# Two graph attention layers, a state space layer and an LSTM in one program: the borders between the layers rearranged

## Time and profile before

| | us |
|---|---|
| median of 3 runs | 4435.55 (4434.5 to 4436.84) |
| profiled execution, its own time | 4431.37 |
| its span | 4429.5 |
| TensorE, VectorE, ScalarE, GpSimd busy | 3978.7, 3492.4, 2881.1, 1199.0 |

### The profile page before, as it was taken

How to read it: one execution, slowest core, us unless ns; L and a number is a source line. 1 busy time by engine, 2 the same in 40 slices (tenths; PEclk the granted TensorE clock), 3 DMA queues, 4 the chain that set the end, 5 groups by cost and what they waited for, 6 DMA issues and landing times. The chain is left out here.

```text
span 4429.5 us, 143416 instructions
## 1 busy us (share of the span) xinstructions
PE 3978.7 (90%) x55570; PEld 2862.1 (65%) x55713; DVE 3492.4 (79%) x9562; ACT 2881.1 (65%) x7050; POOL 1199.0 (27%) x1032
## 2 busy tenths in 40 slices
PE   7999999996999999999997999978888888888882
PEld 4666666653666666666665877767777777777772
DVE  6999999995898889889886888856666666666666
ACT  6999999995888888888885767743333333333330
POOL 4777777862222222222222111000000000000000
PEclk9999999998999999999998999999999999999996
DMA  2222222211000000000002443311121111111115
GB/s 67 79 76 74 77 61 74 77 53 36 25 25 30 30 20 30 30 20 30 30 15 76 145 135 134 128 52 39 36 43 37 43 37 42 39 40 41 38 38 166
DMA packets 327038, 251.03 MB, mean 57 GB/s; under 512 B 172888, under 2 KB 291032, under 8 KB 324312
## 3 DMA queue, kind: packets, MB, share of 16 engines
q1 hardware_dynamic: 324824, 233.40, 18.2%
q10 hardware_dynamic: 1536, 8.39, 0.7%
HBM read 157.27 MB, written 67.12 MB: 51 GB/s over the span
## 5 line engine op out<-in xcount | busy, mean ns | idle before, releaser
L2578 PE MATMUL lstm_G_psum<-next_Whh,lstm_HT 128*32 128x192 f32 x8192 | 439.8, 333 | 238.6 <-DVE lstm_HT L2710 238.6
L2649 ACT ACTIVATE lstm_TC<-lstm_G_psum 128x192 f32<-128x192 f32 x512 | 169.6, 331 | 656.6 <-PE lstm_G_psum L2578 656.6
L1565 ACT ACTIVATE ssm_EX<-ssm_Z_psum,ssm_tok 128x256 f32<-128x256 f32 (+1 forms) x1024 | 371.7, 423 | 156.1 <-PE ssm_Z_psum L1396 86.3
L2570 PE MATMUL lstm_G_psum<-next_Wih,lstm_XT 128*32 128x192 f32 x8192 | 428.1, 327 | 0.0
L2578 PEld LDWEIGHTS lstm_G_psum<-next_Whh,lstm_HT 128*32 128x32 f32 x8192 | 214.4, 109 | 321.1 <-DVE lstm_HT L2710 287.9
L2697 DVE SCALAR_TENSOR_TENSOR lstm_AB<-lstm_TC 128x128 f32<-128x128 f32 x512 | 149.9, 293 | 310.0 <-ACT lstm_TC L2649 307.8
L616 ACT ACTIVATE g_PR<-g_S,g_nmax 128x512 f32<-128x512 f32 x512 | 368.7, 723 | 4.8 <-DVE g_nmax L751 4.8
L758 DVE COPY g_PT<-g_PT_psum 128x512 f32<-128x512 f32 x512 | 344.3, 683 | 25.4 <-PE g_PT_psum L485 20.6
L607 ACT ACTIVATE g_relu<-g_Z_psum,g_src 128x512 f32<-128x512 f32 x512 | 346.5, 684 | 19.3 <-PE g_Z_psum L478 19.3
L2872 POOL TENSOR_SCALAR lstm_rstd<-lstm_mv 128x4 f32<-128x4 f32 x32 | 7.2, 226 | 1277.8 <-DVE lstm_mv L2691 1277.8
L751 DVE CUSTOM_DVE_ANT_0 g_S<-g_Z_psum,g_relu 128x512 f32<-128x512 f32 x512 | 345.1, 683 | 8.8 <-ACT g_relu L607 7.3
(11 more groups left out here) (307 smaller groups left out, 10873.8 us busy)
## 6 DMA issues: line engine op xcount, KB each, us to landing
g_ADJ<-in_adj SPq DMA_DIRECT2D x64, 1024.0 KB, 7.4
x<-g_XO SPq DMA_DIRECT2D x64, 512.0 KB, 5.3
g_X<-in_x SPq DMA_DIRECT2D x32, 512.0 KB, 4.3
ssm_X<-x SPq DMA_DIRECT2D x32, 512.0 KB, 3.8
x<-ssm_OUT SPq DMA_DIRECT2D x32, 512.0 KB, 2.8
g_X<-x SPq DMA_DIRECT2D x32, 512.0 KB, 4.3
lstm_U<-x SPq DMA_DIRECT2D x128, 128.0 KB, 3.5
lstm_V<-lstm_U SPq DMA_DIRECT2D x128, 128.0 KB, 3.2
```

Source lines behind the costliest of these rows:

```text
L1565: ins = act.activation(EX[h % NE][:, col:col + n], Zb[c][:, i * CHUNK:i * CHUNK + n], ACT.Exp, bias=tok[b.slot][:, i, c, h:h + 1])
L2570: pe.matmul(bank[32 * j:32 * (j + 1), 0:n], XT[c.slot][:, kc, :, t], Wih[:, kc, j, first:last], start=False, stop=False, skip_group_check= ...
L2578: ins = pe.matmul(bank[32 * j:32 * (j + 1), 0:last - first], HT[t % 2][:, 32 * kc:32 * (kc + 1)], Whh[:, kc, j, first:last], start=False, ...
L2649: act.activation(TC[t % 2][:, 0:3, :].rearrange("p g e -> p (g e)"), Gb[t % 2][:, 0:IFG], ACT.Tanh).then_inc(s["tg"], 1)
```

## The change

It has five parts.

- `Memory.clear`: the list of semaphores is cut into five, and each engine clears one part.
- Start of the first attention phase: gamma, beta and bias are loaded by `late_tables`, which SP runs after the period of k = -4, that is behind adj of batch 0 and x of batch 1, and counted by the semaphore `late`. TensorE and VectorE wait for `const` >= 32, TensorE for `w` >= 64, GpSimd for neither; GpSimd waits for `late` ahead of the first bias addition. VectorE does `norm_stats` of batch 0 before the weight setup.
- Drain of the first attention phase: for the last batch VectorE, not GpSimd, subtracts the mean (in `residual_sum`) and does the last three passes (`last_layernorm`), behind the copies of WoT.
- Edge check: the sum, the comparison, TensorE's sum and the copy move from the typed phase into the first phase's drain; `any_odd` is a kept tile, and `asked` no longer waits.
- Start of the second attention phase: `norm_stats` of batch 0 before VectorE's wait for the tables.

The phases then have 61, 21, 58, 57 and 40 semaphores.

```diff
@@ Memory.clear
         with self.nc.Block() as block:
+            n = len(self.sems)
+            parts = [self.sems[k * n // 5:(k + 1) * n // 5] for k in range(5)]
+
             @block.gpsimd
             def _(g):
-                for sem in self.sems:
+                for sem in parts[0]:
                     g.sem_clear(sem)
+
+            @block.vector
+            def _(v):
+                for sem in parts[1]:
+                    v.sem_clear(sem)
...
@@ first_attention_phase, sync
-            for tile, name, sem in ((gamma, "gamma", "w"), (beta, "beta", "w"), (bias, "bias", "const")):
-                sp.dma_start(tile[:, :], weights[name].rearrange("(o h) e -> o (h e)", o=1).to_broadcast([P, D])
-                             ).then_inc(s[sem], 16)
+
+            def late_tables():
+                for tile, name in ((bias, "bias"), (gamma, "gamma"), (beta, "beta")):
+                    sp.dma_start(tile[:, :], weights[name].rearrange("(o h) e -> o (h e)", o=1).to_broadcast([P, D])
+                                 ).then_inc(s["late"], 16)
...
             for k in range(-5, nb + 0):
                 period(Batch(None, k, SLOTS))
+                if k == -4:
+                    late_tables()
@@ tensor
-            pe.wait_ge(s["const"], 48)
-            pe.wait_ge(s["w"], 6 * 16)
+            pe.wait_ge(s["const"], 32)
+            pe.wait_ge(s["w"], 4 * 16)
...
             ins.then_inc(s["wo_pe"], 1)
+            pe.wait_ge(s["odd"], 2)
+            pe.matmul(Zb[2][:, 0:1], ones[:, :], odd[:, 1:2], start=True, stop=True).then_inc(s["odd_pe"], 1)
             pe.wait_ge(s["wo"], 2)
@@ vector
+            v.memset(ones[:, :], 1.0).then_inc(s["v"], 1)
+            norm_stats(Batch(None, 0, SLOTS))
-            v.wait_ge(s["const"], 48)
+            v.wait_ge(s["const"], 32)
...
                 v.tensor_reduce(sums[:, :], G[:, :, :].rearrange(heads, h=H), AX, ALU.add).then_inc(s["sum"], 1)
+                if b.off == nb - 1:
+                    Gv = G[:, :, :].rearrange(heads, h=H)
+                    b.wait(v, s["mean"], 1, 1)
+                    v.tensor_tensor(Gv, Gv, bcast(sums[:, :], E), ALU.subtract).then_inc(s["d4"], 1)
...
-                at(b + 1, norm_stats)
+                if b.off >= 0:
+                    at(b + 1, norm_stats)
...
+            v.wait_ge(s["v"], 2)
+            v.wait_ge(s["check"], IT * nb)
+            v.tensor_reduce(odd[:, 0:1], kept["odd"][:, :], AX, ALU.add).then_inc(s["odd"], 1)
+            v.wait_ge(s["odd"], 1)
+            v.tensor_scalar(odd[:, 1:2], odd[:, 0:1], 0.25 * IT * N * nb, None, ALU.is_gt).then_inc(s["odd"], 1)
             v.wait_ge(s["wo_pe"], 1)
             for kc in range(KC):
                 v.tensor_copy(WoT[:, kc, :], Zb[kc][:, :]).then_inc(s["wo"], 1)
+
+            def last_layernorm(b):
+                Gv = G[:, :, :].rearrange(heads, h=H)
+                b.wait(v, s["ln"], 4, 2)
+                v.tensor_tensor(Gv, Gv, bcast(ssq[:, :], E), ALU.mult).then_inc(s["ln"], 1)
+                b.wait(v, s["ln"], 4, 3)
+                v.tensor_tensor(G[:, :, :], G[:, :, :], gamma[:, :].unsqueeze(1).to_broadcast([P, IT, D]),
+                                ALU.mult).then_inc(s["ln"], 1)
+                b.wait(v, s["ln"], 4, 4)
+                b.wait(v, s["xb"], 1, 1)
+                b.dma_wait(v, stored, -1)
+                v.tensor_tensor(XO[b.slot][:, :, :], G[:, :, :], XB[:, :, :], ALU.add).then_inc(s["out"], 1)
+
+            last_layernorm(Batch(None, nb - 1, SLOTS))
+            v.wait_ge(s["odd_pe"], 1)
+            v.tensor_copy(kept["any_odd"][:, :], Zb[2][:, 0:1])
             v.wait_ge(s["wc_pe"], 1)
@@ gpsimd
             g.wait_ge(s["v"], 1)
-            g.wait_ge(s["const"], 48)
-            g.wait_ge(s["w"], 6 * 16)
...
             def bias_added(b):
+                if b.off == 0:
+                    g.wait_ge(s["late"], 48)
...
-                b.wait(g, s["mean"], 1, 1)
-                g.tensor_tensor(Gv, Gv, bcast(sums[:, :], E), ALU.subtract).then_inc(s["d4"], 1)
+                if b.off < nb - 1:
+                    b.wait(g, s["mean"], 1, 1)
+                    g.tensor_tensor(Gv, Gv, bcast(sums[:, :], E), ALU.subtract).then_inc(s["d4"], 1)
...
-                at(b, layernorm, 1)
-                at(b, layernorm, 2)
+                if b.off < nb - 1:
+                    at(b, layernorm, 1)
+                    at(b, layernorm, 2)
-            for k in range(-2, nb + 1):
+            for k in range(-2, nb):
@@ typed_attention_phase
         def asked(eng):
-            eng.wait_ge(s["odd"], 2)
             return eng.value_load(any_odd[0:1, 0:1], min_val=0, max_val=P) > 0
...
@@ second_attention_phase, vector
+            norm_stats(Batch(None, 0, SLOTS))
             v.wait_ge(s["const"], 48)
...
-                at(b + 2, norm_stats)
+                if b.off > -2:
+                    at(b + 2, norm_stats)
```

More of the change, by code:

```diff
@@ L124, in clear, with _ @@
         with self.nc.Block() as block:
+            n = len(self.sems)
+            parts = [self.sems[k * n // 5:(k + 1) * n // 5] for k in range(5)]
             @block.gpsimd
             def _(g):
-                for sem in self.sems:
+                for sem in parts[0]:
                     g.sem_clear(sem)
+            @block.vector
+            def _(v):
+                for sem in parts[1]:
+                    v.sem_clear(sem)
+            @block.scalar
+            def _(act):
+                for sem in parts[2]:
+                    act.sem_clear(sem)
+            @block.tensor
+            def _(pe):
+                for sem in parts[3]:
+                    pe.sem_clear(sem)
+            @block.sync
+            def _(sp):
+                for sem in parts[4]:
+                    sp.sem_clear(sem)
 def bcast(ap, n):
@@ L687, in _, with norm_stats @@
         def _(v):
+            def norm_stats(b):
+                b.dma_wait(v, x_loaded)
+                b.wait(v, s["xn"], IT, 0)
+                for t in range(IT):
+                    ins = v.bn_stats(stats[:, t, :], X[b.slot][:, t, :])
+                ins.then_inc(s["st"], 1)
+                b.wait(v, s["st"], 1, 1)
+                for t in range(IT):
+                    ins = v.bn_aggr(mv[:, t, :], stats[:, t, :])
+                ins.then_inc(s["mv"], 1)
             v.memset(arow[:, :], 0.0).then_inc(s["zero"], 1)
@@ L706, in _ @@
             ins.then_inc(s["setup_v"], 1)
[L708 to L717, removed]
             def make_mask(b, t):
@@ L951, in typed_attention_phase @@
         Eb = m.ps("E")
-        s = {n: m.sem(n) for n in "const odd odd_pe var root loaded v xn xt_pe xt h_pe h right typed z p t ev pv g out stored passed".split()}
+        s = {n: m.sem(n) for n in "const var root loaded v xn xt_pe xt h_pe h right typed z p t ev pv g out stored passed".split()}
         ctx.push(m.clear)
@@ L1071, in steps_done @@
                     def steps_done():
-                        v.wait_ge(s["v"], i * V + (3 + done[0]))
+                        v.wait_ge(s["v"], i * V + (1 + done[0]))
                         v.sem_inc(s["passed"], 1)
@@ L2245, in _, with norm_stats @@
         def _(v):
+            def norm_stats(b):
+                b.dma_wait(v, x_loaded)
+                b.wait(v, s["shift"], 1, 0)
+                for t in range(IT):
+                    ins = v.bn_stats(stats[:, t, :], X[b.slot][:, t, :])
+                ins.then_inc(s["st"], 1)
+                b.wait(v, s["st"], 1, 1)
+                for t in range(IT):
+                    ins = v.bn_aggr(mv[:, t, :], stats[:, t, :])
+                ins.then_inc(s["mv"], 1)
             v.memset(half[:, :], -0.5).then_inc(s["setup_v"], 1)
@@ L2260, in _ @@
             ins.then_inc(s["setup_v"], 1)
-            def norm_stats(b):
-                b.dma_wait(v, x_loaded)
-                b.wait(v, s["shift"], 1, 0)
-                for t in range(IT):
-                    ins = v.bn_stats(stats[:, t, :], X[b.slot][:, t, :])
-                ins.then_inc(s["st"], 1)
-                b.wait(v, s["st"], 1, 1)
-                for t in range(IT):
-                    ins = v.bn_aggr(mv[:, t, :], stats[:, t, :])
-                ins.then_inc(s["mv"], 1)
             def make_mask(b, t):
```

18 lines of the change are left out of this document (5 added, 13 removed).

## The result

The changed kernel takes 4398.92 us (median of 4 runs, 4394.8 to 4400.73) against 4435.24 for the kernel before in the same runs (4434.5 to 4436.84): a ratio of 0.9918, 95% interval 0.9906 to 0.993. The forecast was 4398.5. The profiled execution spans 4397.4 us where the one before spans 4429.5, 32.1 less; the forecast's sum was 37.1. The medians differ by 36.3, the times of the two profiled executions (4431.37 and 4399.52) by 31.9: the one before lay 3.9 us under this median (4.2 under the one that the forecast used), and this one lies 0.6 over its own.

What follows compares the result with a forecast made beforehand. The prediction saw serial load, setup, statistics and normalisation at attention starts, plus drain and border work, as the bound. Gains of 13.8 + 3.6 + 1.5 + 12.3 + 5.9 = 37.1 us gave 4398.5 us (8 in 10: 4389 to 4409).

Steps and rivals of the forecast that it cites:

- start of the first layer: Late tables and early statistics let TensorE start the first batch at 14.95 instead of 28.83 us; gain 13.8 us.
- drain: End of first layer: four element-wise passes move from GpSimd to VectorE at 1.23 us each; gain 3.6 us.
- edge check: First border: the flag is made ahead of the border instead of behind its release; gain 1.5 us.
- branch: Behind the first border: the jumped-over code keeps its length, so TensorE's 3.39 us branch stays; gain 0.
- clears: Five phase ends: semaphores cleared on five engines, 50 in sequence at GpSimd's 0.064 us each; gain 12.3 us.
- second attention start: Statistics begin at 2392.9 instead of 2398.87 us, TensorE's first batch at 2399.8 instead of 2405.74; gain 5.9 us.
- rival 1: First layer: the clock's rise keeps its place instead of moving with the work; up to 6.2 us lost, 4405; 8%.
- 0.14 bound: Borders: upper price in us of one clear on another engine, from TensorE's event wait; clears' gain then 8.5 us.
- rival 3: First layer's drain: GpSimd's x + beta pass makes VectorE's subtraction wait; 2.2 us lost, 4400.7; 20%.
- Shift absorbed: First layer: something that does not move sets its pace and absorbs the start's gain; 4412; 5%.
- slower: First layer's loop: the new load order changes its rhythm; a period 1.2 us longer loses the whole gain; 3%.
- the step that added 4.2 us: Final sum: from 4394.3 for a profiled execution to 4398.5 for the median, as the earlier profile lay 4.2 under its median.

Runs made afterwards that it cites:

- the experiment: Changed kernel with a 128x128 memset ahead of VectorE's last-batch subtraction, so GpSimd's x + beta pass begins first; 4400.1 us (2 runs).
- the last run with them: Changed kernel with range clears and fewer, better placed constant matmuls at the four starts and in both attention setups' gaps; 4382.78 us, ratio 0.9885.
- the earlier one: Changed kernel with 22, 44, 22 and 24 constant matmuls in TensorE's idle time at the four layer starts; 4396.58 us, ratio 0.9911.
- the run with range clears: Changed kernel with a border's semaphores cleared by one GpSimd instruction per range of numbers; 4394.60 us, ratio 0.9905.
- the changed kernel again: Changed kernel with no edit, run for a second profiled execution; 4399.05 us (4 runs).

## Why the prediction came out

The total is right to 0.4 us; its terms are not all.

| step | forecast | measured in the traces |
|---|---|---|
| start of the first layer | 13.8 | 11.3 in one execution, 13.9 in another |
| drain | 3.6 | 3.8 |
| edge check | 1.5 | 1.8; 1.4 when it is undone |
| branch | 0 | within the line above |
| clears | 12.3 | 9.7 alone; 9.9 by the durations in the changed kernel |
| second attention start | 5.9 | 6.5; 6.7 when it is undone |
| clock at the other starts | 0 | -2.0 |
| last stores | 0 | 1.0 |
| sum | 37.1 | 32.1 |

Each part undone, or done alone, costs in its trace what it gave: 4.15 and 8.2 us for the two halves of the start (at the first batch), 3.8 for the drain, 1.4 for the edge check, 6.7 for the second attention layer, and the clears alone give 9.7. Together that is 34 us, against 32.1 with all of them at once, in executions whose clock differs by as much.

- *Start.* The mechanism and the next bound, the setup, are as forecast; the table's landing at 7.0 was met in one execution of the changed kernel (7.08) and missed in the other (7.82, just beyond the forecast's bound of 7.7).
- *Late clock*, rival 1 with 8%: it happened in one profiled execution of the changed kernel's two and cost 1.8 us of its 6.2. It isn't an outcome of the change but a spread between executions: the rise comes 10 to 16 us behind the first batch. As a rival with one price it was posed wrongly.
- *Clears.* The failed term. "I take 12.3, because only TensorE's row is dear" was the right observation and the wrong conclusion: when five engines work side by side the dear one is the time. TensorE's pace, 0.117 us, is near the 0.14 bound worked out from its event wait; with it for the 50 in sequence the forecast would have been 9.7.
- *Edge check, branch.* As forecast: the flag's load moved from 1.6 to 0.1 us behind the release. The stall moves with the branch and keeps about its length; the other 0.3 us of the 1.8 is that TensorE's branch grew by 0.4 while VectorE, last before, now reaches its drain a microsecond ahead of TensorE.
- *Second attention layer.* The statistics went ahead as forecast; the gain is 0.6 larger because GpSimd's first operation no longer runs beside the mask pass.
- *Holding up*, rival 3 with 20%. The two passes do disturb each other, but it is GpSimd's that grows, by 1.0 us, and a lead of 0.1 us didn't help it. The Trainium skill ("SBUF — State Buffer", section "Who interferes with whom") names this pair as contending and lets the one that issues first go first, the other wait. This trace agrees that they contend, and not that the later one waits: VectorE was second in the experiment and took 1.16 us. The drain kept its 3.8 us because GpSimd had 0.2 us to spare.
- *Shift absorbed, slower*: no. The adjacency loads still come 29.9 us apart (24.2 to 921.9 in 30 steps).

The sum was 5.0 us too large for the executions that were profiled. The forecast of the median was saved by the step that added 4.2 us, the distance of one execution from the median, to it: the changed kernel's profiled execution had no such distance. The agreement to 0.4 us is therefore partly luck; what stands on evidence is a gain of 32 to 36 us (31 to 42 by the interval of the ratio).

## What to carry to other kernels

Work that is split over engines ends with the slowest of them: price it by that one, and look first whether one instruction does it all. A layer's first microseconds run at TensorE's lower clock because TensorE waited; matmuls on constants in that wait were worth 9 to 12 us here, nearly as much as the whole rearranged start of the first layer, provided they end before the real work is ready and go on through the gaps of the setup. Two profiled executions of one program differ by up to 3.4 us at a given instruction, so terms of 1 or 2 us are read as differences between neighbouring instructions, not as absolute times or medians.

## What the runs showed of the hardware

- A semaphore clear costs by engine: 0.117 us from one to the next on TensorE (56 ns each), 0.083 on VectorE (54), 0.066 on ScalarE (41), 0.064 on GpSimd (38), 0.058 on SyncE (25 to 30). A clear of a range of 61 takes 0.37 us in all, one of 21 takes 0.15.
- The granted clock after an idle stretch depends on what TensorE did in it: 0.50 without, 1.00 with matmuls on constants, at the starts of layers 2 to 4 in the last run with them (in the earlier one it was 0.64 over 2370 to 2376, at the second attention layer's batch). In the first layer it fell to 0.50 again behind the setup's thin matmuls (64x10) and the rests between them.
- GpSimd's two-input pass over 128x1024 grows from 2.35 to 3.38 or 3.45 us beside one VectorE subtraction of 1.2 us, also from SBUF to SBUF, and its 4-column operation from 0.24 to 0.82 beside VectorE's mask pass.
- Near 340 us one batch of the first layer is disturbed in every trace: VectorE waits 0.9 to 2.3 us for its adjacency load (1.8 in the changed kernel), and TensorE rests for 1.4 to 2.8. In 8 of 13 traces, of kernels of either kind, the clock dips behind that rest, in the others not. Between the kernel before and the one with the clears alone the longer wait made 0.7 us and the dip 1.4. Two stretches of the changed kernel, the rest and the dip:

```profile
330.00:335.00 5.00, 2.42 (x13) 0.80 (x12) 3.24 (x5) 2.77 (x7) 4.21 (x3) 1.00 0.07 27
335.00:340.00 5.00, 4.77 (x18) 2.58 (x20) 4.71 (x14) 3.75 (x9) 0.00 (x0) 0.66 0.01 3
```

The length of the rest doesn't decide it: the run with range clears rests 2.8 us and has no dip, the changed kernel again rests 1.6 and has one. What does stays open.
